# Attention of a hybrid layer in five sessions a head pair: masks written ahead of the products, two units weighted together, row maxima in two-bank groups, outputs copied by ScalarE

## What is computed

```python
kqv = (layernorm(x) @ Wqkv + bqkv).reshape(b, s, 3, 16, 32)      # q, k, v: 16 heads of 32
scores = einsum('bsnh,btnh->bnst', k, q) / sqrt(32)
scores = triu(scores) + -10000.0 * tril(ones, k=-1)
attn = softmax(scores, axis=2)
out = einsum('bnkq,bknh->bqnh', attn, v).reshape(b, s, 512) @ Wo + bo
```

## Time and profile before

| | us |
|---|---|
| median of 3 runs | 3210.86 (3198.68 to 3228.77) |
| span of the profiled execution | 3215.6 |
| granted TensorE clock, mean of the span | 0.963 |

### The profile page before, as it was taken

One profiled execution on the slowest core, in us unless ns is written; L12 is line 12 of the kernel. 1 busy time (PEld: TensorE's weight loads), 2 busy tenths in 40 slices (PEclk: granted clock), 3 DMA queues, 4 the chain that ended last, 5 costly groups with the idle time before them and its releaser, 6 DMA issues.

```text
span 3215.6 us, 59395 instructions
## 1 busy us (share of the span) xinstructions
PE 3021.2 (94%) x20772; PEld 2060.6 (64%) x20772; DVE 2083.9 (65%) x2942; ACT 1119.2 (35%) x1749; POOL 751.5 (23%) x1061
## 2 busy tenths in 40 slices
PE   3899999999999999999989999999998999999998
PEld 3654477777654447777764544877775554677776
DVE  2566565777756665677675666477775666647777
ACT  2133234444123323444322332444421333244442
POOL 3211112334121101333302110133322111023332
PEclk7999999999989999999998999999999999999999
DMA  9322111111232202111132220211123222021112
GB/s 337 83 54 58 28 52 49 50 45 50 73 66 46 66 21 53 46 51 46 38 93 53 66 46 14 66 43 51 38 67 87 46 46 47 14 75 44 52 45 76
DMA packets 163746, 191.55 MB, mean 60 GB/s; under 512 B 43962, under 2 KB 103994, under 8 KB 161786
## 3 DMA queue, kind: packets, MB, share of 16 engines
q1 hardware_dynamic: 157150, 175.83, 20.2%
q10 hardware_dynamic: 6432, 13.63, 1.4%
HBM read 106.99 MB, written 23.36 MB: 41 GB/s over the span
## 4 chain that ended last, share of the span: by engine, by line
PE 77%; DVE 9%; issue 4%; SPq 4%; DMA 4%; ACT 1%; POOL 1%; ACTq 0%; DVEq 0%; POOLq 0%
PE ps L724 14%; PE ps L725 13%; PE ps L726 13%; PE ps L876 8%; PE ps L839 6%; PE ps L859 5%; PE ps L1059 4%; PE ps L943 3%; PE ps L1045 2%; PE ps L1105 2%; PE ps L1068 2%; DMA KS<-EV 2%; DVE mneg L1565 1%; PE ps L734 1%; PE ps L842 1%
## 5 line engine op out<-in xcount | busy, mean ns | idle before, releaser
L724 PE MATMUL ps<-uh,win 128*128 128x512 f32 x1536 | 626.9, 408 | 11.2 <-POOL win L1808 10.5
L725 PE MATMUL ps<-ul,win 128*128 128x512 f32 x1536 | 600.9, 391 | 0.0
L726 PE MATMUL ps<-uh,win 128*128 128x512 f32 x1536 | 600.5, 391 | 0.0
L1565 DVE TENSOR_REDUCE mneg<-ps 128x1 f32<-128x128 f32 (+7 forms) x512 | 363.3, 752 | 168.1 <-PE ps L842 162.7
L1242 ACT ACTIVATE PR<-ps 128x1024 f32<-128x1024 f32 (+3 forms) x384 | 310.1, 809 | 434.8 <-PE ps L862 293.2
L876 PE MATMUL ps<-PR,VG 128*32 128x512 f32 (+3 forms) x1536 | 350.2, 533 | 12.3 <-DVE OS L1571 8.2
L724 PEld LDWEIGHTS ps<-uh,win 128*128 128x128 f32 x1536 | 288.6, 188 | 104.9 <-issue 29.6
L878 PE MATMUL ps<-PR,ones 128*32 128x512 f32 (+3 forms) x1536 | 350.1, 533 | 0.0
L726 PEld LDWEIGHTS ps<-uh,win 128*128 128x128 f32 x1536 | 288.3, 188 | 64.8
L1677 DVE TENSOR_TENSOR LM<-ps,LM 128x512 f32<-128x512 f32 x256 | 170.1, 685 | 242.3 <-PE ps L1059 198.5
L1908 POOL TENSOR_SCALAR_AFFINE_SELECT LM<-LM 128x512 f32<-128x512 f32 x256 | 208.7, 826 | 491.9 <-ACT LM L1318 491.9
(11 more groups left out here) (219 smaller groups left out, 5007.3 us busy)
## 6 DMA issues: line engine op xcount, KB each, us to landing
raw<-in_t SPq DMA_DIRECT2D x128, 256.0 KB, 2.8
QS<-EV SPq DMA_DIRECT2D x192, 128.0 KB, 2.5
KS<-EV SPq DMA_DIRECT2D x168, 128.0 KB, 2.6
in_t<-tiles ACTq DMA_DIRECT2D x10, 1024.0 KB, 8.5
XN<-in_L_attn_a_x_dram SPq DMA_DIRECT2D x40, 256.0 KB, 5.0
win_raw<-in_L_attn_a_Wqkv_dram SPq DMA_DIRECT2D x34, 256.0 KB, 3.4
win_raw<-in_t SPq DMA_DIRECT2D x32, 256.0 KB, 2.7
edec<-ed_t SPq DMA_DIRECT2D x512, 16.0 KB, 1.6
```

Of the source, the lines that this page charges most:

```text
L724: pe.matmul(dst, hi_l, hi_r, start=first, stop=False)
L725: pe.matmul(dst, hi_l, lo_r, start=False, stop=False)
L726: return pe.matmul(dst, lo_l, hi_r, start=False, stop=last)
L1565: dve.tensor_reduce(mneg[:, hh, t:t + 1], wide(b0)[:, 0:(t + 1) * P], AX.X, ALU.max, negate=True).then_inc(a_max.sem, 1)
```

## The change

- A pair's units are taken in five sessions (`SESSIONS`, `WEIGHED`). A session issues on TensorE one group of row tiles for the maxima, then `scores_b` of two units, then a chunk of projections (first four sessions of `hf` 0), a second group of row tiles, and then `weigh` for two units (four in the last session, whose second group is absent and where `turn_maxima` stands ahead of `weigh`). Units 0 and 1 of the next pair follow behind the last session.
- All masks of a group or of two units stand ahead of its products; the first matmul in each bank carries the start flag.
- The maxima are taken in nine groups (`MAX_GROUPS`) of one or two tiles, each 1024 columns in banks 0 and 1. A group waits until the group before it is reduced.
- `PR` has four slots, score banks are 2, 3 and 4, 5 in turn, and `OS` has two halves.
- `take` goes from VectorE to ScalarE, and `invert` is cut into quarters of 128 columns that stand between VectorE's reductions: those of `c` 1 in sessions 0 and 1 of the next pair, those of `c` 0 in sessions 2 and 3.
- ScalarE turns the maxima after the exponentials of units 10 and 11, where it did so after unit 9.
- The loops over groups are written out, and the weights of the next group are loaded a group earlier.

```diff
+WEIGHED = [(0, 1), (2, 3), (4, 5), (6, 7), (8, 9, 10, 11)]
+MAX_GROUPS = [[(0, 7, 0)], [(0, 6, 0), (0, 0, 896)], [(0, 5, 0), (0, 1, 768)], [(0, 4, 0), (0, 2, 640)], [(0, 3, 0), (1, 3, 512)],
+              [(1, 4, 0), (1, 2, 640)], [(1, 5, 0), (1, 1, 768)], [(1, 6, 0), (1, 0, 896)], [(1, 7, 0)]]
+FILLING = [(0, 1), (2, 3), (4, 5), (6, 7), (8,)]
...
+                def group_scores_a(p, slot, occ, j):
+
+                    tiles = MAX_GROUPS[j]
+                    if j in (0, 4):
+                        pe.wait_ge(s_stack[slot][j // 4], occ * 96 + 96)
+                    if j:
+                        a_max.wait(pe, p, sum(len(x) for x in MAX_GROUPS[:j]))
+                    scores_a(slot, tiles)
...
+                        ex.wait(pe, p, max(u - 1, 0))
...
+                        for k in range(SESSIONS):
+                            if ahead:
+                                group_scores_a(p + 1, 1 - hf, occ + hf, FILLING[k][0])
+                            scores_b(p, hf, occ, (2 * k + 2, 2 * k + 3))
+                            if hf == 0 and g < GROUPS - 1 and k < 4:
+                                project(g + 1, k)
+                            if ahead:
+                                for j in FILLING[k][1:]:
+                                    group_scores_a(p + 1, 1 - hf, occ + hf, j)
+                            if k == SESSIONS - 1 and ahead:
+                                turn_maxima(p + 1)
+                            if k == 0:
+                                vg_done.wait(pe, p, 1)
+                            for u in WEIGHED[k]:
                                 weigh(p, hf, u)
...
+                        if ahead:
+                            scores_b(p + 1, 1 - hf, occ + hf, (0, 1))
...
+                            if ahead:
+                                maxima(p + 1, hf, b * 4 + g)
+                            take(p, 1)
...
+                        for k in range(SESSIONS):
+                            for i, j in enumerate(FILLING[k]):
+                                if ahead:
+                                    group_maxima(p + 1, j)
+                                if i == 0 and hf == 0 and g < GROUPS - 1 and k < 4:
+                                    project_lo(g + 1, k, False)
+                                if quarters and quarters[0][0] <= k:
+                                    invert(*quarters.pop(0)[1:])
```

More of the change, by code:

```diff
@@ L264, in hybrid_layer @@
         o_rec = signal("o_rec", 2)
[L265 removed]
+        o_scaled = [signal(f"o_scaled{c}", 1) for c in range(2)]
         z_pe = signal("z_pe", TT)
@@ L824, in project, with scores_a, first_of @@
                     i.then_inc(pj.sem, 1)
-                def scores_a(p, slot, occ, t16):
+                flat = ps[:, 0:4, :].rearrange("p a c -> p (a c)")
+                def scores_a(slot, tiles):
+                    begun = set()
+                    def first_of(at):
+                        new = at // HB not in begun
+                        begun.add(at // HB)
+                        return new
+                    for hh, t, off in tiles:
+                        at = off + t * P
+                        pe.matmul(flat[:, at:at + P], identb[:, :], mask_ts[:, :], start=first_of(at), stop=False, skip_group_check=True)
+                    for hh, t, off in tiles:
+                        n = (t + 1) * P
+                        for c in range(0, n, HB):
+                            m = min(HB, n - c)
+                            i = pe.matmul(flat[:, off + c:off + c + m], QS[slot][0:STACK, hh, t * P:(t + 1) * P],
+                                          KS[slot][0:STACK, hh, c:c + m], start=first_of(off + c), stop=True, skip_group_check=True)
+                        i.then_inc(a_pe.sem, 1)
@@ L836, in scores_a @@
-                    for c in range(0, n, HB):
-                        m = min(HB, n - c)
-                        diag = c + m == n
-                        i = pe.matmul(ps[:, b0 + c // HB, 0:m], QS[slot][0:STACK, hh, t * P:(t + 1) * P],
-                                      KS[slot][0:STACK, hh, c:c + m], start=True, stop=not diag)
-                        if diag:
-                            i = pe.matmul(ps[:, b0 + c // HB, m - P:m], identb[:, :], mask_ts[:, :], start=False, stop=True)
-                    i.then_inc(a_pe.sem, 1)
+                    scores_a(0, [(hh, t, FIRST_MAX_AT[t])])
@@ L1233, in _ @@
                 maxima(b * 8, None, None)
-                for last in (False, True):
-                    with (act.Fori(0, GROUPS - 1) if not last else ExitStack()) as i_:
-                        g = GROUPS - 1 if last else i_
-                        for hf in range(2):
-                            p = b * 8 + g * 2 + hf
-                            for u in range(UNITS):
-                                n = span(u)[3]
-                                st_pe.wait(act, p, u + 1)
-                                act.activation(PR[:, u % 2, :, 0:n], ps[:, SCORE_BANK[u]:SCORE_BANK[u] + 2, 0:n], ACT.Exp, scale=SCALE).then_inc(ex.sem, 1)
-                                if u == TURN_AT and not (last and hf):
-                                    maxima(p + 1, hf, b * 4 + g)
-                                if hf == 0 and not last and u == 1:
-                                    group_hi(b * 4 + g + 1)
-                                if hf == 0 and not last and u - 1 in PROJECT_AT:
-                                    project_hi(g + 1, PROJECT_AT.index(u - 1), False)
+                group_hi(b * 4 + 1)
@@ new lines, in exponentials, with take @@
+                def exponentials(p, u):
+                    n = span(u)[3]
+                    st_pe.wait(act, p, u + 1)
+                    act.activation(PR[:, u % 4, :, 0:n], ps[:, score_bank(u):score_bank(u) + 2, 0:n], ACT.Exp, scale=SCALE).then_inc(ex.sem, 1)
+                def take(p, c):
+                    pv.wait(act, p, 4 if c == 0 else 12)
+                    o_scaled[c].wait(act, p, 0)
+                    act.copy(OS[:, c, :], ps[:, 6, :]).then_inc(o_copied.sem, 1)
+                exponentials(b * 8, 0)
@@ new lines, in _ @@
+                exponentials(b * 8, 1)
+                for g in range(GROUPS):
+                    for hf in range(2):
+                        p = b * 8 + g * 2 + hf
+                        ahead = (g, hf) != (GROUPS - 1, 1)
+                        for k in range(SESSIONS):
+                            for u in (2 * k + 2, 2 * k + 3):
+                                exponentials(p, u)
+                            if hf == 0 and g < GROUPS - 1 and k < 4:
+                                project_hi(g + 1, k, False)
+                            if k == 1:
+                                take(p, 0)
+                                if hf == 1 and g < GROUPS - 2:
+                                    group_hi(b * 4 + g + 2)
+                        if ahead:
+                            maxima(p + 1, hf, b * 4 + g)
+                        take(p, 1)
+                        if ahead:
+                            for u in range(2):
+                                exponentials(p + 1, u)
```

233 lines of the change are left out of this document (105 added, 128 removed).

## The result

The changed kernel takes 3367.8 us (median of 4 runs, 3359.5 to 3374.7) against 3219.8 for the kernel before beside it: 1.049 times, 95% interval 1.045 to 1.053. The forecast was 3305 and the range 3235 to 3400: slower as forecast, by 148 us where 94 were forecast.

What follows compares the result with a forecast made beforehand. TensorE was taken to set the pace, busy 94% of 3215.6 us. Adding 79 (19.7 a sequence, times four) and 15 for clock gave a 3310 us span; the median stands 5 below: 3305, range 3235 to 3400.

Steps and rivals of the forecast that it cites:

- Pairs without projections: Attention, turn to turn of the maxima: stack arrival, then VectorE's chain of nine reductions; 27.0 us against 25.0.
- Pairs with projections: Attention, turn to turn: VectorE's projection split delays the next group, TensorE waits 1.9 us in four sessions; 42.0 us.
- First interval: Start of each sequence's attention: no reciprocals in sessions 0 and 1, fourth projection now inside; 38.2 us against 30.2.
- Last pair: Attention's last pair, no maxima ahead: 16 mask pauses (1.6) and 9 switches (2.9) less; 24.5 becomes 20.0 us.
- Clock: TensorE at half speed behind new waits: 15 us above the 54 lost now, bounds 45 less and 75 more.
- Rival 2: Clock falls in nearly every wait: 138 us more in all, 3428, or 3370 if half is hidden; chance 0.13.
- Outside the attention nothing moves: Everything outside the four attention stretches: no change in time, so the sum was over the turns alone.
- Waits for reductions: TensorE's groups of maxima waiting for VectorE's reductions: 35 to 45 us a sequence, a sign of the forecast.
- Rival 1: TensorE's work decides and waits stay hidden: 21.5 us less a sequence, about 3125 in all; chance 0.10.
- Rival 3: Nothing much changes: stacks 1 us earlier, quarters faster, clock gives back 35 us; 3217; chance 0.10.
- Rival 4: Masks ahead do not save, the pause comes anyway: at most 2 us a sequence more, 3313; chance 0.07.
- The take on ScalarE: Moving take from VectorE to ScalarE: 0.7 us a time, costs nothing, as the stack wait covers it by 2.8 us.

Runs made afterwards that it cites:

- e1: Changed kernel with idle matmuls added: 10 ahead of each pair's stack wait, 6 ahead of the first group of sessions 1 to 4 in projection pairs; 3280.5 us.
- e7: Kernel before with 6 idle matmuls of 512 columns ahead of the first tile of the three pairs a sequence whose stacks come late; 3189.1 us.
- e9: e1 with every quarter of the reciprocals replaced by a plain copy of the same 64 by 128 numbers; 3250.7 us.
- e2: Changed kernel with VectorE taking the reciprocal quarter, then the second group's reductions, ahead of the split of the projection in each session; 3247.9 us.
- e5: e2 with 10 idle matmuls of 512 columns ahead of each pair's stack wait, seven a sequence; 3205.1 us.
- e4: Changed kernel with each mask again behind its own product, everything else as changed; 3427.3 us.
- e11: e5 with the DMAs of head group 1's weights behind the landing of the first pair's stacks instead of ahead; 3192.3 us.
- e8: Kernel before with the two masks ahead of the two products in the score products of the diagonal units; 3199.3 us.
- e3: Changed kernel with session 0 reordered on TensorE: scores of units 2 and 3 and the projection ahead of the first group of maxima; 3364.2 us.

## Why the prediction was right, and where its sizes were off

The direction was right, and so was the mechanism inside the attention. The 151 us between the two spans split so. At full clock a sequence takes 258.7 us from the first turn to the output projection (e1, sequence 1) against 234.8 (e7, sequence 1, the shortest of its four): 23.9 more, 96 in four. The measured four sums are 1121.0 and 993.9; above full clock that is 86 and 55, so clock made 31. Outside lie 24. The filler's own matmuls may lengthen e1's intervals, so 96 is an upper bound and 31 a lower one.

- **Pairs without projections**, forecast 27.0, at full clock 27.7. The stack's arrival 7.8 us after the turn (7.6) and the two nearly equal ways of the groups' chain (e9) hold. Right.
- **Pairs with projections**, forecast 42.0, at full clock 42.7 and 43.6. The cause, VectorE's order, is shown by e2 and e5, which take 5 to 7 us from each of them at full clock, where 4 times 1.9 was counted.
- **First interval**, forecast 38.2 from the start of the window, which is 2.6 us behind the turn in the changed kernel: 41.5 less 2.6 is 38.9. The first three kinds together are 5.8 us a sequence over; the forecast held 2 us for mask distances that are not needed, since masks stand 0.05 apart. That leaves 3.8, which is most of the step from 79 to 96.
- **Last pair**, 20.0 as forecast, but by a wrong split: all 16 mask pauses were counted as saved, 1.6 us, where 11 are, for 0.9 (e4). Not counted were TensorE's waits for exponentials and for the copied outputs, which in sequence 1 fall from 1.94 us (one of 0.29, five of 0.33) to 1.29 (0.94 and 0.35). That leaves about 3.0 for the 9 switches, as forecast (2.9). Two errors of 0.7 cancel, so the exact 20.0 is luck.
- **Clock**, forecast 15, measured 31 or more. This is the term that was mis-sized. The forecast let most waits pass without a fall; in the changed kernel the windows of the pairs that wait stand at 0.85 to 0.88, and the last pair, which does not wait for stacks or reductions, at 1.00. So Rival 2 had the mechanism, a fall behind nearly every wait, but its 138 us are far above 31 (its second figure should be 3359 by its own terms, not 3370). For the 54 us that the kernel before loses to half speed, 993.9 less four times 234.8 gives 55.
- **"Outside the attention nothing moves"** was the step that failed: 24 us. The diff shows an edit on SP that was not priced, the weights of the next group ahead of the row of maxima. In the changed kernel the first tile of a sequence waits 2.2 to 2.3 us for its stack where it waited 1.0 before, 5.0 us in four, and the clock that falls behind it in sequence 0 costs 1.5 more. e11 shows that this is the weights' doing; from e5, where the clock fell behind that wait in all four sequences, it took 13 to 15 us. The other 17.5 of the 24 lie ahead of that tile (14) and behind the last attention (3.5), and no run ties them to an edit: the kernel before with its filler (e7) is 12 us longer outside too.
- **Waits for reductions**, forecast 35 to 45 us a sequence, are 31.5 (126.1 over four). The waits for the stacks, forecast 2.5 to 4 us each, average 2.5.
- **Rival 1** (faster, waits hidden) had its limit at 41 us of these two waits a sequence; they are 51. **Rival 3** (nothing much changes) needed a clock that gives 35 us back, and it took 31. **Rival 4** (masks ahead save nothing) is refuted by e4 and e8. **The take on ScalarE** was costed at nothing and wasn't tried alone.

## What to carry to other kernels

Price a wait twice: its length, and the half-speed stretch behind it; a few idle matmuls in front of an unavoidable wait gained 1.2% in the untouched kernel and 2.6% in the changed one. The clock differs from one execution to the next, so a gain of under 1% should be read from distances at full clock and not from the median alone (e8). When an engine's instructions are put in another order, look at the order of every engine that feeds it: here one line of VectorE's program, the split ahead of the second reductions, was worth 120 us, while the last pair, where the switches and pauses that the change saves show by themselves, gained 4.5 us a sequence. Moving a wait behind other work (e3) gains little when that work has waits of its own.

## What the runs showed of the hardware

- Half speed behind a short wait comes and goes: behind waits of 1.42 us equal pairs took 33.8, 32.3 and 32.3 us in sequence 1 of the kernel before and 29.2 twice in its sequence 0. In e8, without a filler, three waits of 1.7 us in sequence 1 were followed by 29.0 us each, and one such pair in sequence 0 took 40.0. With 6 idle matmuls of 512 columns ahead of the wait (e7) all twelve took 29.2.
- Masks that stand together cost one pause of about 0.1 us for the group and 0.05 us each; masks behind their products cost the pause each time (20.0 against 20.9 us for 16 masks in 5 bunches or behind 16 products).
- A reciprocal of 128 columns on 64 partitions takes 0.936 us, a plain copy of the same 0.233.
- Two loads of weights, 0.5 MB, issued by SP while ScalarE issues the stacks' transfers make these 1.2 us later (2.24 against 1.01 us of waiting).
